# A GNN, attention and mixture-of-experts kernel: gate logits from rows not yet normalised, shorter fillers, one moved low part, and last sums by halves

## What is computed

```python
x = x + gnn(layernorm(x))                       # two graph convolutions
y = layernorm(x)
x = y + attention(ln(y, ln1)) @ Wp + bp          # 12 heads, causal; x is "x2" in the kernel
h2 = (x - mean(x)) * rsqrt(var(x) + 1e-5) * ln2_g + ln2_b
logits = h2 @ Wg                                # 8 experts, the best one of each row is taken
hid = relu(h2 @ W1[e] + b1[e])                  # 768 -> 3072
out = (rows before the FFN part) + x + w * (hid @ W2[e] + b2[e])
```

## Time and profile before

| | |
|---|---|
| median of 3 executions | 882.93 us (882.52 to 887.0) |
| the profiled execution, own time | 885.82 us |
| its span | 884.2 us |
| TensorE busy | 850.2 us (96% of the span) |
| VectorE busy | 715.1 us (81%) |
| ScalarE busy | 552.2 us (62%) |
| GpSimd busy | 78.2 us (9%) |
| HBM traffic | 221 GB/s over the span |

### The profile page before, as it was taken

One profiled execution on the slowest core, in us unless ns is written; L12 is line 12 of the kernel. 1 busy time (PEld: TensorE's weight loads), 2 busy tenths in 40 slices (PEclk: granted clock), 3 DMA queues, 4 the chain that ended last, 5 costly groups with the idle time before them and its releaser, 6 DMA issues.

```text
span 884.2 us, 14643 instructions
## 1 busy us (share of the span) xinstructions
PE 850.2 (96%) x5336; PEld 819.3 (93%) x5336; DVE 715.1 (81%) x1095; ACT 552.2 (62%) x785; POOL 78.2 (9%) x85
## 2 busy tenths in 40 slices
PE   7999999989899998999989999999999999999997
PEld 7889999989789887899979999999999999999996
DVE  6999675873578788665887897998989899898995
ACT  4612342353577777614577787888878788787870
POOL 2000000230400000031600000000000000000040
PEclk9999999999999999999999999999999999999997
DMA  7030008153930033430898999999999999999974
GB/s 218 23 108 1 19 6 174 54 154 75 321 110 2 1 107 103 148 88 1 273 363 309 364 347 375 343 363 372 354 376 359 364 372 357 376 354 372 368 260 130
DMA packets 116232, 196.00 MB, mean 222 GB/s; under 512 B 34052, under 2 KB 83420, under 8 KB 116182
## 3 DMA queue, kind: packets, MB, share of 16 engines
q1 hardware_dynamic: 107988, 169.08, 56.6%
q0 software_dynamic: 6368, 24.19, 8.0%
q10 hardware_dynamic: 1826, 2.06, 0.9%
HBM read 177.40 MB, written 17.90 MB: 221 GB/s over the span
## 4 chain that ended last, share of the span: by engine, by line
PE 56%; DVE 21%; DMA 12%; ACT 5%; issue 5%; SPq 0%; DVEq 0%; ACTq 0%
PE ps L1486 12%; DVE wlo L994 11%; DMA raw<-in_L_ffn_W 11%; PE ps L1900 10%; PE ps L1881 9%; PE ps L1663 7%; PE ps L1739 3%; PE ps L1717 2%; PE ps L1567 2%; PE ps L1593 2%; PE ps L1702 2%; ACT whi L664 2%; PE ps L1515 2%; PE ps L1866 1%; DMA xs<-in_x 1%
## 5 line engine op out<-in xcount | busy, mean ns | idle before, releaser
L994 DVE TENSOR_TENSOR wlo<-raw,whi 128x2304 fp32r<-128x2304 f32 (+1 forms) x150 | 352.8, 2360 | 21.6 <-ACT whi L664 20.9
L664 ACT ACTIVATE whi<-raw 128x2304 fp32r<-128x2304 f32 (+1 forms) x152 | 300.7, 1979 | 82.4 <-DMA raw<-in_L_ffn_W 30.6
L1900 PE MATMUL ps<-whi,hTT 128*128 128x384 f32 x768 | 202.7, 340 | 1.0 <-ACT oh7T L664 1.0
L1900 PEld LDWEIGHTS ps<-whi,hTT 128*128 128x128 f32 x768 | 140.3, 189 | 1.2 <-ACT oh7T L664 1.2
L1881 PE MATMUL ps<-whi,hgh 128*128 128x384 f32 x384 | 133.2, 347 | 1.3 <-DVE hgl L994 1.3
L1900 PE MATMUL ps<-wlo,hTT 128*128 128x384 f32 x384 | 129.7, 338 | 0.0
L1881 PE MATMUL ps<-whi,hgl 128*128 128x384 f32 x384 | 129.1, 336 | 0.0
L1881 PE MATMUL ps<-wlo,hgh 128*128 128x384 f32 x384 | 128.4, 334 | 0.0
L1881 PEld LDWEIGHTS ps<-whi,hgh 128*128 128x128 f32 x384 | 72.2, 188 | 1.5 <-DVE hgl L994 1.5
L1900 PEld LDWEIGHTS ps<-wlo,hTT 128*128 128x128 f32 x384 | 72.8, 190 | 0.0
L1881 PEld LDWEIGHTS ps<-wlo,hgh 128*128 128x128 f32 x384 | 72.3, 188 | 0.0
(11 more groups left out here) (291 smaller groups left out, 1627.6 us busy)
## 6 DMA issues: line engine op xcount, KB each, us to landing
raw<-in_L_ffn_W SPq DMA_DIRECT2D x128, 1152.0 KB, 6.9
hs_d<-bc POOLq DMA_DIRECT2D x13, 384.0 KB, 6.4
raw<-in_L_gnn_W SPq DMA_DIRECT2D x4, 1152.0 KB, 6.3
hs<-hs_d POOLq DMA_DIRECT2D x8, 384.0 KB, 5.5
ys_d<-ysb POOLq DMA_DIRECT2D x7, 384.0 KB, 6.0
raw<-in_L_ffn_Wv SPq DMA_DIRECT2D x6, 384.0 KB, 5.4
raw<-in_L_ffn_Wq SPq DMA_DIRECT2D x12, 192.0 KB, 3.7
raw<-in_L_ffn_Wk SPq DMA_DIRECT2D x12, 192.0 KB, 3.4
```

Of the source, the lines that this page charges most:

```text
L664: act.activation(out_, in_, func).then_inc(s, 1)
L994: dve.tensor_tensor(out_, in_, hi_, ALU.subtract).then_inc(s, 1)
L1900: ins = mm(ps[0:CAP, 4 + half, 0:HB], l, rr, start=k == 0 and j == 0 and jj == 0, stop=k == FCH - 1 and j == JW - 1 and jj == 2)
```

## The change

The mean and the deviation of a row are no longer applied ahead of the gate products. `x2` is turned and multiplied by `wgs`; the column sums of `wgs` come from a second set of six products in the front (with a column of ones), and VectorE afterwards makes (product − mean × column sum) × deviation + bias. `n2` is still made, for the picks and the scatter. On ScalarE the copies of a block now stand ahead of the root of the next, those of both last blocks ahead of the last root. Fillers: 14 and 4 are dropped, 8 become 6, 12 become 9. `split_lo(0, 0)` moves from ahead of the ranks to behind `oh0`; `split_lo(2, 0)` moves behind the first tile's low parts. In the tail blocks 0 to 2 are made half by half, final sums are by halves in the order of `FIN_ORDER`, the fifth block of other experts' rows is added behind the low halves, and rows 112 to 124 are stored from ScalarE's queue.

```diff
+FIN_ORDER = ((0, 0), (1, 0), (2, 0), (0, 1), (1, 1), (2, 1), (3, 0), (3, 1), (4, 0), (4, 1))
-NORM_BUSY, GATE_BUSY, RANK_BUSY, CHOICE_BUSY = 14, 4, 8, 12
+RANK_BUSY, CHOICE_BUSY = 6, 9
...
@@ sync @@
             for c in range(C):
-                sp.wait_ge(s_fin, c + 1)
-                for r0, r1 in PARTS:
-                    sp.dma_start(tok(out)[r0:r1, c, :], base[r0:r1, c, :]).then_inc(s_out, 16)
+                sp.wait_ge(s_fin, FIN_ORDER.index((c, 1)) + 1)
+                r0, r1 = PARTS[0]
+                sp.dma_start(tok(out)[r0:r1, c, :], base[r0:r1, c, :]).then_inc(s_out, 16)
@@ gpsimd @@
+            gp.memset(one[:, :], 1.0).then_inc(s_const, 1)
@@ scalar @@
             for c in range(C):
+                if c:
+                    h2_turned(c - 1)
+                if c == C - 1:
+                    h2_turned(c)
                 root_of()
-                if c >= 1:
-                    h2_turned(c - 1)
-            h2_turned(C - 1)
...
+            for c in range(C):
+                a.wait_ge(s_fin, FIN_ORDER.index((c, 1)) + 1)
+                r0, r1 = PARTS[1]
+                a.dma_start(tok(out)[r0:r1, c, :], base[r0:r1, c, :]).then_inc(s_out, 16)
@@ vector @@
-            dve.tensor_copy(gbias[:, :], ps[0:P, 6, 0:E]).then_inc(s_gbr, 1)
+            dve.tensor_copy(gbias[:, :], ps[0:P, 6, 0:2 * E]).then_inc(s_gbr, 1)
...
+            d.wait_ge(s_gbr, 1)
+            step(dve.tensor_tensor(shift_, down(mv2[:, :, 0]), across(gbias[:, E:2 * E]), ALU.mult))
             d.wait_ge(s_gate, 1)
-            step(dve.tensor_tensor(lg, ps[0:P, 2, 0:C * E].rearrange("p (c e) -> p c e", e=E),
-                                   gbias[:, :].rearrange("p (o e) -> p o e", o=1).broadcast_to((P, C, E)), ALU.add))
+            step(dve.tensor_tensor(lg, ps[0:P, 2, 0:C * E].rearrange("p (c e) -> p c e", e=E), shift_, ALU.subtract))
+            step(dve.tensor_tensor(lg, lg, down(rstd2[:, :]), ALU.mult))
+            step(dve.tensor_tensor(lg, lg, across(gbias[:, 0:E]), ALU.add))
...
-            split_lo(0, 0)
             d.wait_ge(s_rank, 1)
...
             d.wait_ge(s_oh0, C)
+            split_lo(0, 0)
...
             split_lo(1, 0)
-            split_lo(2, 0)
             d.wait_ge(s_eh, 1)
             lo(hg[1][:, 0:EARLY, :], hgf[:, 0:EARLY, :], hg[0][:, 0:EARLY, :], s_el)
             d.wait_ge(s_hgh, 1)
             lo(hg[1][:, EARLY:DC, :], hgf[:, EARLY:DC, :], hg[0][:, EARLY:DC, :], s_hgl)
+            split_lo(2, 0)
...
+            for c in range(C - 1):
+                others_y(c)
             for half in range(2):
                 d.wait_ge(s_yh, half + 1)
...
+            others_y(C - 1)
             d.wait_ge(s_yin, C)
-            for c in range(C):
-                d.wait_ge(s_sel, c + 1)
-                bv = base[:, c, :].rearrange("p (a b) -> p a b", a=2)
-                dve.scalar_tensor_tensor(bv, wide(LAST_BANK[c], P), wtok[:, c:c + 1], bv,
+            for n, (c, half) in enumerate(FIN_ORDER):
+                d.wait_ge(s_sel, n + 1)
+                bv = base[:, c, half * HB:(half + 1) * HB]
+                dve.scalar_tensor_tensor(bv, ps[0:P, LAST_BANK[c] + half, 0:HB], wtok[:, c:c + 1], bv,
                                          ALU.mult, ALU.add).then_inc(s_fin, 1)
@@ tensor @@
+            pe.wait_ge(s_wgs, 1)
+            for m in range(DC):
+                ins = mm(ps[0:P, 6, E:2 * E], one[:, :].broadcast_to((128, P)), wgs[:, m, :], start=m == 0, stop=m == DC - 1)
             ins.then_inc(s_gb, 1)
...
-            def turn_n2(c):
-                pe.wait_ge(s_n2, c + 1)
+            def turn_x2(c):
+                pe.wait_ge(s_x2, c + 1)
...
             held = front_w[1][0]
-            keep_busy(NORM_BUSY, held[:, 0:128], held[:, 0:512], 3)
-            turn_n2(C - 1)
+            turn_x2(C - 1)
             gate_products(C - 2)
-            keep_busy(GATE_BUSY, held[:, 0:128], held[:, 0:512], 3)
             gate_products(C - 1).then_inc(s_gate, 1)
...
             pe.wait_ge(s_oh0, C)
+            pe.wait_ge(s_n2, C)
...
-            for c in range(3):
-                for half in range(2):
-                    bias_y(c, half)
-            pe.wait_ge(s_yl, 1)
-            for c in range(3):
-                spread_y(c, 0)
-            pe.wait_ge(s_yl, 2)
-            for c in range(3):
-                spread_y(c, 1).then_inc(s_sel, 1)
-            for c in range(3, C):
-                if c == C - 1:
-                    pe.wait_ge(s_fin, 1)
-                for half in range(2):
-                    bias_y(c, half)
-                    ins = spread_y(c, half)
-                ins.then_inc(s_sel, 1)
+            for half in range(2):
+                for c in range(3):
+                    bias_y(c, half)
+                pe.wait_ge(s_yl, half + 1)
+                for c in range(3):
+                    spread_y(c, half).then_inc(s_sel, 1)
+            for c in range(3, C):
+                for half in range(2):
+                    if c == C - 1:
+                        pe.wait_ge(s_fin, FIN_ORDER.index((0, half)) + 1)
+                    bias_y(c, half)
+                    spread_y(c, half).then_inc(s_sel, 1)
```

More of the change, by code:

```diff
@@ L135, in build @@
         wgs = sb("wgs", [128, DC, E], F32)
-        gbias = sb("gbias", [P, E], F32)
+        gbias = sb("gbias", [P, 2 * E], F32)
+        one = sb("one", [128, 1], F32)
+        mv2 = sb("mv2", [P, C, 2], F32)
+        rstd2 = sb("rstd2", [P, C], F32)
         bc = [sb(f"bc{i}", [128, D], F32) for i in range(2)]
@@ L148, in build @@
         mv = sb("mv", [P, 2], F32)
-        rstd = sb("rstd", [P, 1], F32)
         var = sb("var", [P, C], F32)
@@ L376, in build @@
             "probs_turned", "probs_hi", "probs_lo", "heads_done", "heads_hi", "heads_lo"))
-        s_wp, s_x2, s_base, s_n2, s_n2T, s_h2T, s_gate = (sem(n) for n in (
-            "attn_projected", "x2_made", "base_made", "n2_made", "n2_turned", "h2T_made", "gates_done"))
+        s_wp, s_x2, s_base, s_n2, s_x2T, s_h2T, s_gate = (sem(n) for n in (
+            "attn_projected", "x2_made", "base_made", "n2_made", "x2_turned", "h2T_made", "gates_done"))
         s_wgs, s_gb, s_gbr = sem("gate_weights_scaled"), sem("gate_bias_done"), sem("gate_bias_read")
@@ L888, in h2_turned @@
             def h2_turned(c):
-                a.wait_ge(s_n2T, c + 1)
+                a.wait_ge(s_x2T, c + 1)
                 for m0, m1 in ((0, 4), (4, DC)):
@@ L977, in _ @@
             with a.If(n_over > 0):
-                a.wait_ge(s_fin, C)
+                a.wait_ge(s_fin, 2 * C)
                 with a.Fori(0, K_OVER) as s:
@@ L1023, in _, with norm @@
             rsqrts = [0]
-            def norm(out_, in_):
+            def norm(c, out_, in_):
                 dve.bn_stats(stats[:, 0, 0, :], in_[:, 0:HB])
                 step(dve.bn_stats(stats[:, 0, 1, :], in_[:, HB:D]))
-                step(dve.bn_aggr(mv[:, :], stats[:, 0, :, :]))
-                rsqrt(mv[:, 1:2], EPS, ALU.add, rstd[:, :], 1)
-                return dve.tensor_scalar(out_, in_, mv[:, 0:1], rstd[:, :], ALU.subtract, ALU.mult)
+                step(dve.bn_aggr(mv2[:, c, :], stats[:, 0, :, :]))
+                rsqrt(mv2[:, c, 1:2], EPS, ALU.add, rstd2[:, c:c + 1], 1)
+                return dve.tensor_scalar(out_, in_, mv2[:, c, 0:1], rstd2[:, c:c + 1], ALU.subtract, ALU.mult)
             step(dve.memset(ps[:, 4:6, 0:HB], 0.0))
@@ L1075, in _ @@
                     step(last)
-            d.wait_ge(s_const, 8)
+            d.wait_ge(s_const, 9)
             dve.tensor_copy(onesr[:, :], onesb[:, :]).then_inc(s_ones, 1)
@@ L1306, in _ @@
                 d.wait_ge(s_x2, c + 1)
-                norm(n2[:, c, :], x2[:, c, :]).then_inc(s_n2, 1)
+                norm(c, n2[:, c, :], x2[:, c, :]).then_inc(s_n2, 1)
+            across = lambda v_: v_.rearrange("p (o e) -> p o e", o=1).broadcast_to((P, C, E))
+            down = lambda v_: v_.rearrange("p (c o) -> p c o", o=1).broadcast_to((P, C, E))
+            shift_ = rt[:, 9, 8:8 + C * E].rearrange("p (c e) -> p c e", e=E)
+            d.wait_ge(s_gbr, 1)
+            step(dve.tensor_tensor(shift_, down(mv2[:, :, 0]), across(gbias[:, E:2 * E]), ALU.mult))
             d.wait_ge(s_gate, 1)
@@ L1439, in _, with others_y @@
             d.wait_ge(s_base, C)
-            for c in range(C):
+            def others_y(c):
                 d.wait_ge(s_yg[c], 16)
@@ L1455, in _ @@
             with d.If(n_over > 0):
-                d.wait_ge(s_fin, C)
+                d.wait_ge(s_fin, 2 * C)
                 with d.Fori(0, K_OVER) as s:
@@ L1518, in _ @@
                 if i == min(TURN_X):
-                    pe.wait_ge(s_const, 8)
+                    pe.wait_ge(s_const, 9)
                 if i in TURN_X:
@@ L1784, in turn_n2 @@
                 for m in range(DC):
-                    ins = nc.tensor.transpose(blocks(0, 128, DC, P)[:, m, :], n2[:, c, m * 128:(m + 1) * 128],
```

(6 more changed lines are left out.)

3 lines of the change are left out of this document (1 added, 2 removed).

## The result

The changed kernel took 889.29 us in the median of 20 executions (883.85 to 896.84), the kernel before 883.37 us in 20 (879.27 to 887.22): ratio 1.0062, 95% interval 1.0042 to 1.0082. It is slower, by 5.9 us where 2.8 were forecast, and lies at the very end of the range. The spread has doubled: the standard deviation of the 20 times is 3.8 us against 1.8.

What follows compares the result with a forecast made beforehand. TensorE, busy for 96% of the span, was taken to bound the kernel, with VectorE and weight transfers leading in places. Front +3.5, gates after give-back −0.4 and tail −0.3 sum to +2.8: 885.7 us, range 880.3 to 889.3.

Steps and rivals of the forecast that it cites:

- the first product for queries: Sign in the front: it starts 2.0 us later than before, with the clock behind it at 0.50 for some 3.4 us.
- The logits: Sign in the gates: they are read some 8 us behind the last projection, against 9.3 before.
- the ranks: Sign behind the gates: they are read 2.4 us earlier against the last projection than before.
- The stall: Sign in the first tile: TensorE's wait around 458 us is as long as or longer than before, ended by a chunk.
- One sign of being wrong: In the gates: the prediction is wrong if the last root does not stand on the path of the logits.
- Term A: Front: waiting for wgs and six more products delay the queries 2.0 us, half clock adds 1.5; +3.5 us.
- Term B: Gates to `oh0`: gate products from x2, and no low part ahead of the ranks, gain time; −2.4 us.
- the middle between two bounds: Gates to `oh0`: −2.4 us, taken between −4.2 and −0.6, as the clock's fall comes between 406 and 410.
- The bound of −0.6: Gates to `oh0`: with half clock from the turn on, logits are read at 413.3 and ranks at 418.3; −0.6 us.
- The third rival: Gates: half clock begins with the turns of x2, the first tile's stall grows; +4.6 us, 887.5 us; chance 0.23.
- Term C: First tile: the new order of low parts delays the loads of chunks 5 to 7, giving back 2.0 us.
- Term D: Tail: half-row last sum −0.47, one store issue less −0.38, two more product changes +0.5; −0.3 us, bounds +3 and −1.7.

Runs made afterwards that it cites:

- e1_front: Kernel before plus the front's column sums of wgs, made ahead of the queries and not used; 887.73 us, ratio 1.0024 to the kernel before.
- e4_gates: Changed kernel with the tail and the order of low parts of the kernel before; 888.03 us, ratio 1.0052 to the kernel before.
- e2_low: Kernel before with only the order of the low parts of chunks 0 and 2 changed; 883.28 us, ratio 1.0003 to the kernel before.
- e5_late: Changed kernel with the column sums moved behind the four groups of query and key products; 885.5 us, ratio 1.0004 to the kernel before.
- e12_bestlow: e8_best with the change's order of the low parts; 883.83 us, ratio 1.0002 to the kernel before.
- e3_tail: Kernel before with only the change's tail; 883.24 us, ratio 0.9982 to the kernel before.
- e6_fill: Changed kernel with all four sets of fillers back at 14, 4, 8 and 12; 889.27 us, ratio 1.0046 to the kernel before.
- e11_nofill: e8_best with the change's fillers (none, none, 6 and 9); 883.19 us, ratio 0.9998 to the kernel before.
- e8_best: Changed kernel with later sums, old low-part order, last root ahead of last copies, fillers 4, 2, 8, 12; 883.54 us, ratio 0.9985 to kernel before.

## Why the prediction was right, and where not

The direction and the range were right, but the range only by luck: 889.29 against an upper end of 889.3, and slower by over 0.5% had been given 0.18. The last 1.8 us of the range stood for a half-clock stretch in the tail; the loss came from longer ones in the front and the gates. Of the signs named in advance, the first product for queries starts 4.2 us behind the bias products in the changed profile (217.50 − 213.29) and 1.2 before, 3.0 us later instead of 2.0. The logits come 9.3 us behind x2 instead of 8, the ranks 0.2 us earlier against it instead of 2.4. The last sum takes 0.62 us and the span ends 4.4 us after it starts, instead of 0.55 and 3.6. The stall is longer and ends by a chunk, as said. One sign of being wrong did show: the last root does not stand on the path of the logits.

**Term A, +3.5: held.** e1_front measured +3.4 with the wait, the products and the half clock where they were put. The seven profiles with the sums ahead of the queries give the pieces: 2.2 us for wait and products (forecast 2.0) and 1.5 to 1.6 for each 3.4 us at half (forecast 1.5). What was off is the length: the clock stood at half for 6.8 to 6.9 us in three of them, for 3.4 in three, and not at all in one. What makes the same instructions pay in some executions and not in others, no run here shows.

**Term B, −2.4: this step failed.** e4_gates less e1_front gives +0.4, and e2_low's −0.4 brings in B's other part, the low part off the ranks' path, with its price in C: about nothing, where the prediction had −0.4 for B and C together and −2.4 for B. The gain exists with a full clock: e4_gates' profiled execution read the logits 2.7 us sooner against x2. The fall came about where it was put: 2.9 to 5.9 us behind x2 of the last block in the six profiles that have it there with these gates, where 406 to 410 meant 1.6 to 5.6. But the middle between two bounds was the wrong choice. The bound of −0.6 already let the half clock last from the last turn through the rank products, and charged nothing behind them. It lasted 17 us in the changed kernel and 13.6 us in e5_late, while TensorE did gate products, 6 and 9 fillers, rank products and picks. The third rival, the half clock from the turns on, is nearest to the profiled execution, and still too mild: `oh0` starts 15.2 us behind x2 instead of 15.4, and the picks 18.1 instead of 16.5. The fillers ahead of the picks, costed at nothing, are part of this: 9 took 4.19 us. Whether it is the turns or the gate products of 8 columns beside them that let the clock fall, no run here separates. The working has a slip too: its terms add up to ranks read at 414.05 and 417.8, where it goes on with 414.65 and 418.3; the middle would have been −2.9, further off.

**Term C, giving back 2.0 of B: borne out by the profiles, not by the times.** The profiles give 2.0 us from the picks to the second expert, as it says. The gain of the same move, the low part of chunk 0 off the ranks' path, is counted in B; alone it is 1.7 us at the ranks and 1.1 at the picks (e2_low). In the times alone the order shows nothing (e2_low, e12_bestlow); in the changed kernel it is some 2 us by means that overlap.

**Term D, −0.3:** e3_tail measured −1.3, within the bounds, with an interval that includes a ratio of 1; the sign is not shown.

The parts measured alone sum to 3.8 (front and gates together, e4_gates) − 0.4 − 1.3 = +2.1 by the means, the whole is +5.7. The standard error of this difference is about 2 us, so the 3.6 that are left are within twice that. They may be chance, or come where parts meet: marks that are late by the clock, and loads that hang on low parts behind the marks. This stays open.

## What to carry to other kernels

A filler on TensorE cost here what it was longer than the wait that it filled: 14 in a gap of 1 us, and 4 more behind them, cost 2.7 us (e6_fill against e4_gates). Before dropping one, price not only the work beside it but the whole run of small products that follows: without fillers it stayed at half clock for 13.6 us instead of 3.4 and the logits came 2.2 us later (e11_nofill against e8_best). Small products that feed something much later belong into a gap of the chain, not ahead of its next dense group: the same six products shifted the last block by 2.2 to 5.4 us in one place and by 1.0 to 2.0 us in the other. When executions of one kernel differ by 10 us, compare the clock of each execution before comparing medians. And where times are too noisy, compare one stretch between two fixed instructions over all profiles: here one such stretch agreed within 0.15 us where the times of one kernel spread over 6 us and more.

## What was not expected of the hardware

The clock stayed at 0.50 for 17 us in which the profile shows TensorE busy for all 17.00 (414 to 431): here a stretch that is full in the profile was at half clock from end to end. And one kernel's time followed its clock over executions closely enough to estimate a price: 0.41 us for each us at half in the changed kernel. That is less than the 0.45 that the ratio of 1.83 between weight loads, 0.33 us at 0.50 and 0.18 at 1.00, would give for dense work; that part of it falls into waits is a guess. In the kernel before, the same fit over 35 executions gives 0.34 with a correlation of only 0.54.
